# A chunk's expert worked out by division on SyncE, its first biases copied by VectorE, and the combination's offset added in pieces

## What is computed

```python
# layer 2
logits = (x @ gate_w + gate_b) / TEMP
topk_vals, topk_idx = jax.lax.top_k(logits, TOP_K)          # TOP_K = 2 of E = 8
h = gelu(einsum('bsd,edf->bsef', x, w1) + b1)               # D = 128, F = 512
expert_out = einsum('bsef,efd->bsed', h, w2) + b2
out = einsum('bse,bsed->bsd', gate_probs, expert_out)
out = (out - mu) / sqrt(var + EPS) * ln_g + ln_b            # ln_b is the "offset"
x = x + tanh(g_ffn[2]) * out
# layer 3: the first cap = 1280 tokens of an expert count, the rest is dropped
h = silu(xe @ W1) * (xe @ W3)
ye = h @ W2
```

## Time and profile before

| | |
|---|---|
| median of 3 runs | 1522.02 us (1521.98 to 1524.61) |
| profiled execution, its own time | 1530.68 us |
| span of its trace | 1528.9 us |
| busy share of the span: TensorE, VectorE, GpSimd, ScalarE | 76%, 63%, 55%, 51% |
| mean granted clock of TensorE | 0.887 |
| second layer's experts: first transpose to last product | 788.22 to 946.64 us |
| third layer's experts: first transpose to last product | 1295.93 to 1496.83 us |

### The profile page before, as it was taken

One profiled execution on the slowest core, in us unless ns is written; L12 is line 12 of the kernel. 1 busy time (PEld: TensorE's weight loads), 2 busy tenths in 40 slices (PEclk: granted clock), 3 DMA queues, 4 the chain that ended last, 5 costly groups with the idle time before them and its releaser, 6 DMA issues.

```text
span 1528.9 us, 39431 instructions
## 1 busy us (share of the span) xinstructions
PE 1168.2 (76%) x12350; PEld 983.7 (64%) x12350; DVE 960.3 (63%) x2996; ACT 784.5 (51%) x2054; POOL 837.9 (55%) x1103
## 2 busy tenths in 40 slices
PE   2888882972888859877438987598888972999991
PEld 1666762861776647656438887366666662999991
DVE  3788882217899967668732222488778874555554
ACT  2676661321788835455226665566555651333333
POOL 0365766342777713375754443576888885333334
PEclk9999995895899989978559999699999995999996
DMA  5222310734233266051126666500000301677775
GB/s 144 88 101 95 95 40 29 208 116 138 98 110 100 72 267 233 12 174 38 52 69 178 179 178 179 141 2 2 16 17 17 102 23 43 210 233 229 227 227 166
DMA packets 144391, 177.76 MB, mean 116 GB/s; under 512 B 18986, under 2 KB 94268, under 8 KB 144192
## 3 DMA queue, kind: packets, MB, share of 16 engines
q1 hardware_dynamic: 133504, 154.22, 32.9%
q0 software_dynamic: 10688, 21.06, 4.0%
HBM read 119.16 MB, written 57.23 MB: 115 GB/s over the span
## 4 chain that ended last, share of the span: by engine, by line
PE 26%; POOL 8%; issue 7%; DVE 6%; SPq 4%; DMA 3%; ACT 3%; POOLq 0%; DVEq 0%; ACTq 0%
PE l3e_ps_h L1502 4%; PE l3e_ps_h L1504 4%; PE l3e_ps_y L1513 4%; POOL l_rows_in L1080 3%; DMA l2e_rows<-l_rows_in 2%; PE l2e_ps_h L1502 2%; PE l3a_ps_kv L2546 2%; PE l3a_ps_ym L2617 2%; PE l2e_ps_y L1513 1%; POOL l3a_cms L2439 1%; PE l3a_ps_q L2530 1%; SPq L1483 1%; SPq L1468 1%; DVE x L686 1%; POOL l3a_nvt L2456 1%
## 5 line engine op out<-in xcount | busy, mean ns | idle before, releaser
L1549 ACT ACTIVATE l3e_sT<-l3e_ps_h 128x128 f32<-128x128 f32 x284 | 78.8, 278 | 134.2 <-PE l3e_ps_h L1504 129.9
L1594 POOL DMA_INDIRECT l_rows_out<-l3e_y,l3e_target x71 | 68.8, 970 | 137.9 <-DVE l3e_y L1577 131.7
L1546 ACT ACTIVATE l2e_hT<-l2e_ps_h,l2e_b 128x128 f32<-128x128 f32 x284 | 101.2, 368 | 83.8 <-PE l2e_ps_h L1502 72.3
L1558 DVE TENSOR_TENSOR l3e_hT<-l3e_sT,l3e_ps_h 128x128 f32<-128x128 f32 x284 | 81.8, 288 | 85.3 <-ACT l3e_sT L1549 70.5
L1594 POOL DMA_INDIRECT l_rows_out<-l2e_y,l2e_target x71 | 68.9, 971 | 91.9 <-DVE l2e_target L1571 79.4
L1502 PE MATMUL l2e_ps_h<-l2e_xT,l2e_w 128*128 128x128 f32 x568 | 111.5, 280 | 0.5 <-DVE l2e_xT L1565 0.5
L1502 PE MATMUL l3e_ps_h<-l3e_xT,l3e_w 128*128 128x128 f32 x568 | 111.0, 277 | 0.5 <-DVE l3e_xT L1565 0.5
L1504 PE MATMUL l3e_ps_h<-l3e_xT,l3e_w 128*128 128x128 f32 x568 | 110.6, 277 | 0.0
L1513 PE MATMUL l2e_ps_y<-l2e_w,l2e_hT 128*128 (+1 forms) x568 | 110.2, 277 | 0.0
L1513 PE MATMUL l3e_ps_y<-l3w_w,l3e_hT 128*128 (+1 forms) x568 | 109.3, 275 | 0.0
L1502 PEld LDWEIGHTS l2e_ps_h<-l2e_xT,l2e_w 128*128 128x128 f32 x568 | 89.6, 199 | 0.8 <-DVE l2e_xT L1565 0.8
(11 more groups left out here) (550 smaller groups left out, 3756.4 us busy)
## 6 DMA issues: line engine op xcount, KB each, us to landing
l3e_w<-in_L_ffn_W SPq DMA_DIRECT2D x142, 256.0 KB
l2e_w<-in_L_ffn_w SPq DMA_DIRECT2D x79, 256.0 KB, 4.4
l_rows_in<-l1f_empty SPq DMA_DIRECT2D x34, 528.0 KB, 7.4
l1a_side<-in_fside_Bx16xSxS SPq DMA_DIRECT2D x32, 512.0 KB, 3.5
l0e_w<-in_L_ffn_w SPq DMA_DIRECT2D x32, 256.0 KB, 3.1
l_rows_in<-l0a_fill_rows SPq DMA_DIRECT2D x15, 528.0 KB, 2.7
l_rows_out<-l0a_fill_rows SPq DMA_DIRECT2D x12, 512.0 KB, 3.6
l2e_rows<-l_rows_in SPq DMA_DIRECT2D x71, 66.0 KB
```

Source lines behind the costliest of these rows:

```text
L1546: nc.scalar.activation(hT[:, q % 2, f, :], ps_h[f][:, 0:SLOTS], act_func, **bias).then_inc(sems["h_ready"], 1)
L1549: nc.scalar.activation(sT[:, f, :], ps_h[f][:, 0:SLOTS], act_func).then_inc(sems["s_ready"], 1)
L1558: nc.vector.tensor_tensor(hT[:, q % 2, f, :], sT[:, f, :], ps_h[f][:, SLOTS:2 * SLOTS], ALU.mult).then_inc(sems["h_ready"], 1)
L1594: pool.indirect_dma_start(out=r.rows_out, out_offset=bass.IndirectOffsetOnAxis(ap=target[:, q % RING:q % RING + 1], axis=0), in_=y[:, q % ...
```

## The change

- **SyncE.** `first`, the chunk's first row, is loaded before the weights are fetched, and the expert is `first // stride`. So a chunk takes one load in place of two. For this the place has to name the expert for every chunk: chunks that hold nothing now point at the last 128 rows of expert 7 (`E * stride - SLOTS`) and no longer at E * stride, and layer 3's stride becomes cap + 128 = 1408, so that those rows are spare.
- **ScalarE** reads its bias from `b1c`, a ring of four small tiles. It loads nothing and waits for neither the weights nor `allotted`.
- **VectorE** loads the expert in `copy_x` (once a chunk, as before, and kept in `chosen` for `b2`), copies the four bias columns into `b1c` (128 x 4), then copies the rows. Both copies count on `xT_ready`.
- **Offset.** `Combine.shift` is split. `gain` stays ahead of the experts. The sum over `x` is made in eight pieces of 128 x 512, after `stored` in turns 16 to 23 of the second layer's experts.

```diff
-        self._step(dve, V.tensor_scalar(self.line[:, :], self.line[:, :], float(SLOTS), float(E * self.stride), ALU.add, ALU.min))
+        self._step(dve, V.tensor_scalar(self.line[:, :], self.line[:, :], float(SLOTS), float(E * self.stride - SLOTS), ALU.add, ALU.min))
...
+    b1c = ph.sb("b1c", [P, RING, FC]) if b1_dram is not None else None
+    per_x = 2 if b1_dram is not None else 1
...
     def sync(sp, rows_ready, allotted):
-        def load_first(q):
-            e, k = expert_of(sp, q), q % ROWS
+        def load_first(q, e):
+            k = q % ROWS
             freed(sp, "h_ps", (q - ROWS + 1) * FC)
             sp.dma_start(w1[:, k, :], w1_dram[e, :, :]).then_inc(sems[f"in{k}"], 16)
             if w3 is not None:
...
         for q in range(ROWS):
-            load_first(q)
+            load_first(q, q)
         rows_ready(sp)
         for q in range(N):
             if q == E:
                 sp.wait_ge(allotted, 1)
+            if q < E:
+                first, e = q * stride, q
+                tile = r.rows_in[first:first + SLOTS, :]
+            else:
+                first = sp.value_load(r.chunk_base[0:1, q - E:q - E + 1], min_val=0, max_val=E * stride - SLOTS)
+                e = first // stride
+                tile = r.rows_in[bass.ds(first, SLOTS), :]
             if q >= ROWS:
-                load_first(q)
-            if q < E:
-                tile = r.rows_in[q * stride:q * stride + SLOTS, :]
-            else:
-                first = sp.value_load(r.chunk_base[0:1, q - E:q - E + 1], min_val=0, max_val=r.rows_in.shape[0] - SLOTS)
-                tile = r.rows_in[bass.ds(first, SLOTS), :]
+                load_first(q, e)
             freed(sp, "y_ready", 2 * (q - ROWS + 1))
             sp.dma_start(rows[:, q % ROWS, :], tile).then_inc(sems[f"in{q % ROWS}"], 16)
...
-            freed(pe, "xT_ready", q - 1)
+            freed(pe, "xT_ready", per_x * (q - 1))
...
-                passed(pe, "xT_ready", q + 1)
+                passed(pe, "xT_ready", per_x * (q + 1))
...
-    def scalar(act, allotted):
+    def scalar(act):
         nc.scalar.preload_act_table(act_func)
-        if b1 is not None:
-            passed(act, "w_in", 16 * w_dmas)
         for q in range(N):
-            if b1 is not None:
-                if q == E:
-                    act.wait_ge(allotted, 1)
-                e = expert_of(act, q)
             for f in range(FC):
                 passed(act, "h_ps", q * FC + f + 1)
                 if w3 is None:
                     if f == 0:
                         freed(act, "y_ps", q - 1)
-                    bias = {"bias": b1[:, columns(e, FC, f, 1)]} if b1 is not None else {}
+                    bias = {"bias": b1c[:, q % RING, f:f + 1]} if b1 is not None else {}
                     nc.scalar.activation(hT[:, q % 2, f, :], ps_h[f][:, 0:SLOTS], act_func, **bias).then_inc(sems["h_ready"], 1)
...
-    def vector(dve, allotted):
+    def vector(dve, allotted, between=None):
+        chosen = {}
+
...
         def copy_x(q):
             if not is_chunk(q):
                 return
+            if b1 is not None:
+                if q == E:
+                    dve.wait_ge(allotted, 1)
+                chosen[q] = expert_of(dve, q)
+                freed(dve, "h_ready", (q - RING + 1) * FC)
+                nc.vector.tensor_copy(b1c[:, q % RING, :], b1[:, columns(chosen[q], FC, 0, FC)]).then_inc(sems["xT_ready"], 1)
             passed(dve, "xT_ps", q + 1)
             freed(dve, "h_ps", (q - 1) * FC)
             nc.vector.tensor_copy(xT[:, q % 2, :], ps_x[q % 2][:, 0:SLOTS]).then_inc(sems["xT_ready"], 1)
@@ -1571,14 +1577,12 @@
             nc.vector.tensor_copy(target[:, q % RING:q % RING + 1], rows[:, q % ROWS, D:D + 1]).then_inc(sems["y_ready"], 1)
             passed(dve, "y_ps", q + 1)
             if b2 is not None:
-                e = expert_of(dve, q)
-                nc.vector.tensor_tensor(y[:, q % RING, :], ps_y[q % 2][:, 0:D], b2[:, columns(e, D, 0, D)], ALU.add).then_inc(sems["y_ready"], 1)
+                nc.vector.tensor_tensor(y[:, q % RING, :], ps_y[q % 2][:, 0:D], b2[:, columns(chosen.pop(q), D, 0, D)], ALU.add).then_inc(sems["y_ready"], 1)
...
         if b2 is not None:
             passed(dve, "w_in", 16 * w_dmas)
-            dve.wait_ge(allotted, 1)
...
             stored(q - 1)
+            if between is not None:
+                between(q)
...
-    def shift(self, dve):
+    def gain(self, dve):
 
         V, s = self.nc.vector, self.s
         dve.wait_ge(s["lnp_in"], 32)
         for k in range(2):
             V.tensor_scalar(self.lnp[:, k, :], self.lnp[:, k, :], self.core.gates[:, self.gate:self.gate + 1], None, ALU.mult).then_inc(s["gated"], 1)
-        dve.wait_ge(s["gated"], 2)
-        V.tensor_tensor(self.core.x[:, :, :], self.core.x[:, :, :], self.lnp[:, 1, :].unsqueeze(1).broadcast_to([P, NT, D]), ALU.add
-                        ).then_inc(s["shifted"], 1)
+
+    def shift(self, dve, q):
+
+        if not self.is_quad(q):
+            return
+        at = slice(4 * q, 4 * q + 4)
+        dve.wait_ge(self.s["gated"], 2)
+        self.nc.vector.tensor_tensor(self.core.x[:, at, :], self.core.x[:, at, :], self.lnp[:, 1, :].unsqueeze(1).broadcast_to([P, 4, D]), ALU.add
+                                     ).then_inc(self.s["shifted"], 1)
...
-        pool.wait_ge(s["shifted"], 1)
+        pool.wait_ge(s["shifted"], q + 1)
...
-    router = Router(nc, ph, core, r, wr_dram, cap, cap=cap, clamp=1e4)
+    router = Router(nc, ph, core, r, wr_dram, stride, cap=cap, clamp=1e4)
...
+        stride = cap + SLOTS
...
         third, third_weights, third_stored, _, _ = slotted_programs(
-            nc, core, Part(phase, "l3e", "right"), held, r3, cap, a["L3_ffn_W1"], a["L3_ffn_W2"],
+            nc, core, Part(phase, "l3e", "right"), held, r3, stride, a["L3_ffn_W1"], a["L3_ffn_W2"],
...
             pairs.vector(dve)
-            combine.shift(dve)
-            expert.vector(dve, allotted)
+            combine.gain(dve)
+
+            def shift(q):
+                combine.shift(dve, q - 16)
+            expert.vector(dve, allotted, between=shift)
```

More of the change, by code:

```diff
@@ L1604, in psum_free @@
     def psum_free(pe):
-        passed(pe, "xT_ready", N)
+        passed(pe, "xT_ready", per_x * N)
         passed(pe, "h_ready", N * FC)
         passed(pe, "y_ready", 2 * N)
-    end = {"w_in": 16 * w_dmas, "xT_ps": N, "xT_ready": N, "h_ps": N * FC, "h_ready": N * FC, "y_ps": N, "y_ready": 2 * N}
+    end = {"w_in": 16 * w_dmas, "xT_ps": N, "xT_ready": per_x * N, "h_ps": N * FC, "h_ready": N * FC, "y_ps": N, "y_ready": 2 * N}
     end.update({f"in{k}": per_chunk * len(range(k, N, ROWS)) for k in range(ROWS)})
@@ L2301, in pair_programs, with linear_programs @@
     return Programs(sync, tensor, scalar, vector, gpsimd), rows_sent, psum_free, done, router.s["allotted"]
-def linear_programs(nc, core, ph, before, gate, wq_dram, wkv_dram, null_kv, lnq_g, lnq_b, lno_g, lno_b, wout_dram, r, wr_dram, cap, route_gate):
+def linear_programs(nc, core, ph, before, gate, wq_dram, wkv_dram, null_kv, lnq_g, lnq_b, lno_g, lno_b, wout_dram, r, wr_dram, stride, cap, route_gate):
     HD = 64
@@ L2952, in pairs_to_end @@
             a["L3_xattn_ln_q_b"], a["L3_xattn_ln_out_g"], a["L3_xattn_ln_out_b"], a["L3_xattn_Wout"],
-            r3, a["L3_ffn_Wr"], cap, 7)
+            r3, a["L3_ffn_Wr"], stride, cap, 7)
         own.release_psum()
@@ L2991, in _ @@
             pairs.scalar(act)
-            expert.scalar(act, allotted)
+            expert.scalar(act)
             attention.scalar(act)
-            third.scalar(act, third_allotted)
+            third.scalar(act)
             last.scalar(act)
```

## The result

The changed kernel takes 1498.66 us (median of 4 runs, 1496.45 to 1500.72) against 1523.32 (1521.98 to 1526.43, 4 runs) before: a ratio of 0.9835, with a 95% interval of 0.9813 to 0.9858. That is 24.7 us less. The profiled execution took 1499.28, its span is 1497.5. Of all executions on record one, of a later experiment, ran in a slow state (1666.65 us at a mean granted clock of 0.711, where the others have 0.87 to 0.90) and is left out of every figure.

A forecast was written before the change was run, and what follows sets the result against it. It took SyncE's own instruction time in the second layer's experts as the bound. Gains of 3.6 (router's scatter), 19.5 (experts' turns) and 2.0 (stage's end) made 25.1 us, from 1522.02 to 1497; range 1493 to 1510, held at some 0.9.

The forecast's parts named there:

- What bounds the kernel: Second layer's experts: SyncE's own instruction time holds TensorE's turn at 2.215 us; freed, it becomes 1.90, 19.5 us gained.
- The turns of the first chunks: Second layer's experts, the eight first chunks: they had no loads before and gain nothing.
- The division: SyncE's step from first row to expert, shown by no trace row: up to 0.15 us, bounds 0 to 0.66.
- The scatter: Router's last scatters: VectorE's sum over all of x holds one up on the path; moving it returns 3.6 us.
- Rival 3: Router's last scatters: the sum did not hold the long one, so 3.6 us stay, 1500.6 us; chance 0.04.
- The end of the stage: After TensorE's last product: the next attention's weights, issued relatively earlier, no longer end last; 2.0 us gained, ends 0 and 2.7.
- The pieces: Offset's sum in turns 16 to 23: 0.55 us each, hidden, at no cost; 4.4 us if nothing covers it.
- The bias copy: VectorE's new 128 x 4 copy, 71 times: 0.14 us each, hidden in slack; 10 us if uncovered.
- Rival 4: VectorE's bias copy falls behind GpSimd's scatter in every chunk and ends with it: 36 us slower, 1554; chance 0.03.
- The sum: Whole kernel: 3.6 + 19.5 + 2.0 = 25.1 us gained, median becoming 1497 us.

The follow-up runs named there:

- the run with that part alone: The kernel before with only the offset changed: gain ahead of the experts, the sum in eight pieces in turns 16 to 23; 1520.09 us, ratio 0.9977.

## Why the prediction was right, point by point

**What bounds the kernel.** Right, and shown by four runs: with SyncE's part alone TensorE's turn is its own 1.90, with two more divisions still 1.90, with the second load back without its checks 2.06 and with them 2.31. 19.5 us were forecast for the 62 turns, 62 x (2.215 - 1.902) = 19.4 came. The turns of the first chunks, which were to gain nothing, became 1.3 us shorter in the profile (one wait of the third turn); why was not tried.

**The division.** It was the open price, taken as 0 to 0.15 within bounds of 0 to 0.66; it is 0.05, and SyncE's turn 1.67 within the 1.62 to 1.77 forecast.

**The scatter.** Forecast 3.6, measured 3.5 in the profile; the times of the run with that part alone, 2.6 less, can't be told from nothing, as its pieces stand in a loop that SyncE still paces. That the sum holds the scatter up is shown: when the sum moves away the scatter takes 0.97, and where the whole sum lies in turn 16 the scatter there takes 4.40 and ends 0.85 behind the sum. Rival 3 falls. The trace disagrees with the probe told of in the Trainium skill (SBUF — State Buffer, Who interferes with whom), in which such an operation did not hold up GpSimd's transfers: 4.40 and 4.55 us here beside 0.97. The section's other sentence, that an operation with both inputs in SBUF contends with GpSimd's reads, may still be what happens; whether the scatter reads through that port, no run here shows.

**The end of the stage.** The term that was mis-sized: forecast 2.0, measured 1.3 (2.72 to 1.39). SyncE's last rows went out 9.65 us ahead of TensorE's end (forecast 9.9), and the last transfer of weights holds VectorE for only 0.20 us, as forecast. But a wait that was not named took the place of the old one: late landings of earlier scatters hold the last targets' copies. Its size changes from run to run: with SyncE's part alone the end got longer (3.54), and the changed kernel run again, on another chip, has 2.85 and 2.21, by which the gain would be nothing or 0.5. So the mechanism of this term was half right, and its 1.3 is one reading among these. Both attempts to move the weights took the end down to about 0.4, which speaks for these transfers as what delays the scatters, and neither was faster. The run with the late bias copy has 0.35 too, with the weights where they were but a slower loop, in which they were issued 10.4 us ahead of TensorE's end and not 9.2.

**The pieces.** Forecast hidden, and hidden: 0.68 us each and not 0.55, `xT` 0.40 ahead of its need. The run without the bias part shows how near the edge this is: with the load no longer under the piece they cost 1 us.

**The bias copy.** Forecast 0.14 and hidden; it took 0.17 and is hidden. The part as a whole was put at nothing; by the profile of the run without it, it saves 1.0 us in the turns with a piece and 0.6 at the stage's end, which the times could not confirm. Rival 4 was priced too high. Its premise, that a copy started inside a scatter waits for its end whenever it starts, is wrong: it waits only in the last 0.46 us of the 0.97.

**The sum.** 25.1 forecast, 24.7 measured. The two terms that carry it are right, 3.6 and 19.5 against 3.5 and 19.4. That the whole agrees within 0.4 is luck: the end gave less than forecast, the first chunks 1.3 that were put at nothing, and two medians of the changed kernel on one chip lie 2.8 apart.

## What to carry to other kernels

Add up what one engine that only issues transfers spends on its own instructions in a turn (loads of registers, checks, issues), and compare it with the turn of the engine that should be the bound; a steady beat on the one and scattered waits on the other is the sign. Leave it a few tenths of a us below: 0.2 were enough here (1.71 against 1.90), and just above, the loss was 9.5 us where the medians said 1.2. A vector operation over a whole tensor beside GpSimd's indirect transfers belongs into pieces that each fit under a wait that is there anyway, and one long stop of TensorE cost its length again at the lower clock here.

## What the runs showed of the hardware that had not been expected

- An integer division by a constant on SyncE costs 0.05 us, a further one with a multiplication 0.02, beside 0.27 for a register load and 0.2 for its checks.
- A 128 x 4 copy within SBUF on VectorE is held by GpSimd's indirect transfer only in the last 0.46 us of its 0.97; one that starts earlier in it takes its usual 0.17.
- The issue of a transfer on SyncE, 0.33 us as a rule, now and then takes up to 1.7 us; in the run with two loads nine took 0.76 to 1.51, about every 13 us. What it waits for, no run here told.
- After a stop of 3.3 us TensorE's granted clock was 0.52 for 6 us, having been 1.00 ahead of it, in the run with the whole sum in turn 16.
